# Three complement masks of a head made by adding transfers, and a new order of source tiles on the matmul engine

## The reference, cut to what matters

```python
seq = (x @ W_seq).reshape(N, H, DH)                    # N 2048, H 16, DH 32
scores = score1[:, :, None] + score2[:, None, :]
scores = leaky_relu(scores, negative_slope=0.2)
scores = scores + (1.0 - adj)[None, :, :] * MASK_VAL   # MASK_VAL -65500
attn = softmax(scores, axis=-1)
hidden = einsum('hij,jhd->ihd', attn, seq).reshape(N, D_IN)
```

## Time and profile before

| | |
|---|---|
| median of 3 runs | 1165.29 us (1164.87 to 1166.19) |
| the profiled execution | 1169.42 us, its span 1167.0 us |
| PE busy | 1080.7 us (93%) |
| DVE busy | 949.3 us (81%) |
| ACT busy | 809.0 us (69%) |
| POOL busy | 163.1 us (14%) |
| bytes moved | 77.69 MB, mean 67 GB/s |

### The profile page before, as it was taken

How to read it: one execution, slowest core, us unless ns; L and a number is a source line. 1 busy time by engine, 2 the same in 40 slices (tenths; PEclk the granted TensorE clock), 3 DMA queues, 4 the chain that set the end, 5 groups by cost and what they waited for, 6 DMA issues and landing times. The chain is left out here.

```text
span 1167.0 us, 24746 instructions
## 1 busy us (share of the span) xinstructions
PE 1080.7 (93%) x10565; PEld 738.8 (63%) x10565; DVE 949.3 (81%) x1323; ACT 809.0 (69%) x843; POOL 163.1 (14%) x174
## 2 busy tenths in 40 slices
PE   1999986999999999999996999999999999999997
PEld 1444432444444444444443999999999999999743
DVE  2355336899999999998834899999999999999565
ACT  1334326677777777775525999999999999999122
POOL 2788640000000000000000100100110000000011
PEclk9999996999999999999997899999999999999999
DMA  9630452322221121000433011110111111111311
GB/s 340 142 26 2 110 104 68 75 57 66 66 66 43 42 57 57 28 37 27 163 126 131 38 38 38 38 39 38 38 38 38 39 38 38 38 39 38 110 72 72
DMA packets 38269, 77.69 MB, mean 67 GB/s; under 512 B 5653, under 2 KB 15250, under 8 KB 36114
## 3 DMA queue, kind: packets, MB, share of 16 engines
q1 hardware_dynamic: 31954, 67.62, 16.1%
q0 software_dynamic: 6208, 8.50, 6.0%
HBM read 65.39 MB, written 23.21 MB: 76 GB/s over the span
## 5 line engine op out<-in xcount | busy, mean ns | idle before, releaser
L1443 ACT ACTIVATE area_h<-area_a,keep 128x2048 fp8e4<-128x2048 f32 x208 | 396.9, 1987 | 0.5 <-PEq L1577 0.5
L1595 PE MATMUL psum<-s_V,area_h 128*128 128x99 bf16 x2560 | 254.5, 210 | 21.1 <-issue 10.9
L1595 PEld LDWEIGHTS psum<-s_V,area_h 128*128 128x128 fp8e4 x2560 | 237.4, 98 | 25.2 <-issue 22.8
L1598 PE MATMUL psum<-s_V,area_h 128*128 128x198 bf16 x1536 | 218.7, 249 | 0.0
L1599 PE MATMUL psum<-s_V,late 128*128 128x99 bf16 x1536 | 212.8, 209 | 0.0
L1596 PE MATMUL psum<-s_V,area_b 128*128 128x99 bf16 x2048 | 205.5, 210 | 0.0
L1596 PEld LDWEIGHTS psum<-s_V,area_b 128*128 128x128 fp8e4 x2048 | 190.3, 98 | 0.0
L737 PE MATMUL psum<-area_h,f_region 128*128 128x512 f32 x384 | 184.9, 596 | 0.0
L1493 DVE TENSOR_TENSOR area_h<-area_h,area_a 128x512 uint32<-128x512 uint32 x256 | 173.5, 688 | 9.1 <-ACT area_h L1443 4.6
L1159 DVE SCALAR_TENSOR_TENSOR f_region<-area_b,s_r,f_region 128x1500 f32<-128x1500 f32 x96 | 170.8, 1780 | 2.2
L1170 DVE CUSTOM_DVE_ANT_0 area_b<-psum,late 128x1500 f32<-128x1500 f32 x96 | 161.1, 1715 | 10.8 <-PE psum L652 10.6
(11 more groups left out here) (175 smaller groups left out, 1343.5 us busy)
## 6 DMA issues: line engine op xcount, KB each, us to landing
area_a<-s_rows SPq DMA_DIRECT2D x16, 1024.0 KB, 4.6
rel_planes<-f_h SPq DMA_DIRECT2D x3, 2304.0 KB, 15.9
late<-rel_planes SPq DMA_DIRECT2D x36, 192.0 KB, 2.6
area_h<-in_x SPq DMA_DIRECT2D x4, 1024.0 KB, 12.9
keep<-in_adj POOLq DMA_DIRECT2D x16, 256.0 KB, 6.6
f_region<-in_x SPq DMA_DIRECT2D x16, 256.0 KB, 4.7
x<-f_region SPq DMA_DIRECT2D x16, 256.0 KB, 2.0
area_a<-adj_chunks SPq DMA_DIRECT2D x4, 1024.0 KB, 9.1
```

Of the source, the lines that this page charges most:

```text
L1443: act.activation(masks[:, j, :], s1b[:, b, :], ACT.Relu, bias=t["s2"][:, n, 0, j:j + 1], scale=BIG, saturate=False).then_inc(signs, 1)
L1595: pe.matmul(out[:, :, 0:DZ], masks[:, j, cols], V[:, b, j, :, 0:DZ], **first)
L1598: pe.matmul(out, masks[:, j, cols], V[:, b, j, :, :], **first)
```

## The change

Tiles 1, 6 and 10 get their complement from transfers. For each, and each head: SP copies the adjacency tile from a new DRAM tensor `far_rows` into the complement's buffer, once PE has used that buffer (`begin_far`); POOL, when DVE has masked the tile and that copy has landed, issues a transfer with addition that adds the mask onto it as 16-bit integers. In bytes 0x40 + 0x40 is 0x80, the fp8 value -0, and 0x40 + 0 stays 2.0, so what is left is the adjacency less the mask. For head 0 DVE makes the copies, and SP stores them from there into `far_rows`, ahead of stage 4.

FAR grows from 10 tiles to 12: 4 and 10 are new in it. DVE's complements are 0, 4, 7, 9, 11, 13, 14 (seven, before eight: 0, 1, 6, 7, 9, 11, 13, 14); POOL's stay 3 and 5. NEAR tiles are 2, 8, 12, 15 (before also 4 and 10), so `nadjT` has four tiles. PE takes the tiles in the order of `TURN`; ACT's and DVE's order stays 0 to 15, with waits for the place of a tile in `TURN`.

```diff
@@ stage 2, SP @@
+            for d, j in enumerate(DMA_FAR):
+                sp.wait_ge(t["apart"], d + 1)
+                sp.dma_start(t["far_rows"][d], t["fars"][FAR.index(j)]).then_inc(t["far_begun"][d], 16)
@@ stage 2, DVE, behind the loop of nadjT @@
+            for j in DMA_FAR:
+                dve.tensor_scalar(t["fars"][FAR.index(j)].bitcast(U32).rearrange("p (t i) -> p t i", t=NT),
+                                  t["adjT"][:, :, j, :].bitcast(U32), 0, None, ALU.bitwise_or).then_inc(t["apart"], 1)
@@ constants @@
-FAR = (0, 1, 3, 5, 6, 7, 9, 11, 13, 14)
+FAR = (0, 3, 4, 5, 7, 9, 11, 13, 14, 1, 6, 10)
 POOL_FAR = (3, 5)
-VECTOR_FAR = tuple(j for j in FAR if j not in POOL_FAR)
+DMA_FAR = (1, 6, 10)
+VECTOR_FAR = tuple(j for j in FAR if j not in POOL_FAR + DMA_FAR)
+TURN = (0, 2, 3, 4, 5, 7, 1, 8, 9, 11, 6, 12, 13, 14, 15, 10)
@@ stage 4, SP @@
-            for n in range(HB - 2):
-                sp.wait_ge(mask_ready, NT * (n + 1))
-                load(n + 2, n % 2)
+            def begin_far(n, d):
+                place = TURN.index(DMA_FAR[d])
+                if place < NT - 1:
+                    sp.wait_ge(mask_used, (NT - 1) * (n + 1) + place + 1)
+                else:
+                    sp.wait_ge(psum_done[1], n + 1)
+                sp.dma_start(fars[FAR.index(DMA_FAR[d])], t["far_rows"][d]).then_inc(far_begun[d], 16)
+            for n in range(HB - 1):
+                for d in range(len(DMA_FAR) - 1):
+                    begin_far(n, d)
+                if n < HB - 2:
+                    sp.wait_ge(mask_ready, NT * (n + 1))
+                    load(n + 2, n % 2)
+                begin_far(n, len(DMA_FAR) - 1)
@@ stage 4, POOL @@
-                for j in POOL_FAR:
+                for j in sorted(POOL_FAR + DMA_FAR):
                     pool.wait_ge(mask_ready, NT * n + j + 1)
-                    complement(pool, j, ALU.subtract).then_inc(pool_far, 1)
+                    if j in POOL_FAR:
+                        complement(pool, j, ALU.subtract).then_inc(pool_far, 1)
+                    else:
+                        d = DMA_FAR.index(j)
+                        pool.wait_ge(far_begun[d], 16 * (n + 1))
+                        pool.dma_start(fars[FAR.index(j)].bitcast(U16), masks[:, j, :].bitcast(U16), accum_op=ALU.add).then_inc(far_added[d], 16)
@@ stage 4, ACT (and the same in vector_sign on DVE) @@
-                        if j < NT - 1:
-                            act.wait_ge(mask_used, (NT - 1) * n + j + 1)
+                        if TURN.index(j) < NT - 1:
+                            act.wait_ge(mask_used, (NT - 1) * n + TURN.index(j) + 1)
@@ stage 4, PE @@
-            def step(n, b, half, j):
-                base = 4 * half
+            def step(n, b, half, place):
+                base, j = 4 * half, TURN[place]
                 if j in POOL_FAR:
                     pe.wait_ge(pool_far, len(POOL_FAR) * n + POOL_FAR.index(j) + 1)
+                elif j in DMA_FAR:
+                    pe.wait_ge(far_added[DMA_FAR.index(j)], 16 * (n + 1))
```

More of the change, by code:

```diff
@@ L21 @@
 U8 = mybir.dt.uint8
+U16 = mybir.dt.uint16
 F8 = mybir.dt.float8e4
@@ L1389, in stage4 @@
     pool_far = sem("pool_far")
+    far_begun = t["far_begun"]
+    far_added = [sem(f"far_added{d}") for d in range(len(DMA_FAR))]
     summed, scaled, joined, inverse = sem("summed"), sem("scaled"), sem("joined"), sem("inverse")
@@ L1481, in vector_sign @@
             def vector_sign(n, b, j):
-                dve.wait_ge(mask_used, (NT - 1) * n + j + 1)
+                dve.wait_ge(mask_used, (NT - 1) * n + TURN.index(j) + 1)
                 dve.wait_ge(s1_in[b], 8 * (n - b) + 16)
@@ L1577, in _ @@
             pe.sem_inc(mask_used, NT - 1)
-            def step(n, b, half, j):
-                base = 4 * half
-                if j == 0:
+            def step(n, b, half, place):
+                base, j = 4 * half, TURN[place]
+                if place == 0:
                     pe.wait_ge(bank_free[half], n + 1)
@@ L1591, in step @@
                     out = ps[:, base + i // 2, 256 * (i % 2):256 * (i % 2) + 3 * CZ].rearrange("p (s c) -> p s c", s=3)
-                    first = dict(start=(j == 0 and i % 2 == 0), stop=False, skip_group_check=True)
-                    then = dict(start=False, stop=(j == NT - 1), skip_group_check=True)
+                    first = dict(start=(place == 0 and i % 2 == 0), stop=False, skip_group_check=True)
+                    then = dict(start=False, stop=(place == NT - 1), skip_group_check=True)
                     if j in FAR:
@@ L1599, in step @@
                         last = pe.matmul(out[:, :, DZ:CZ], nadjT[:, NEAR_TILES.index(j), cols], V[:, b, j, :, DZ:CZ], **then)
-                if j == NT - 1:
+                if place == NT - 1:
                     last.then_inc(psum_done[half], 1)
-                if half and j < NT - 1:
+                if half and place < NT - 1:
                     last.then_inc(mask_used, 1)
@@ L1735, in build @@
         "s1_rows": dram("s1_rows", [HB, N]), "seq_rows": dram("seq_rows", [N, D]),
-        "adj_chunks": dram("adj_chunks", [NT, P, N], F8),
+        "adj_chunks": dram("adj_chunks", [NT, P, N], F8), "far_rows": dram("far_rows", [len(DMA_FAR), P, N], F8),
     }
@@ L1746, in build @@
         t["adjT_in"], t["seq_in"] = (c.enter_context(nc.semaphore(n)) for n in ("adjT_in", "seq_in"))
+        t["apart"] = c.enter_context(nc.semaphore("apart"))
+        t["far_begun"] = [c.enter_context(nc.semaphore(f"far_begun{d}")) for d in range(len(DMA_FAR))]
         t["rstd"] = c.enter_context(nc.sbuf_tensor("rstd", [P, 2, NT], F32))
```

## The result

Twenty executions each: median 1170.88 us after (1165.02 to 1173.84) against 1166.12 before (1160.47 to 1171.62); the medians differ by 4.8 us. The ratio, which is that of the means, is 1.0031 with a 95% interval of 1.0016 to 1.0047, so 3.6 us slower (1.9 to 5.5). Forecast were 1.1 us faster. The profiled executions are 1170.67 us after (span 1168.9) and 1169.42 before (1167.0).

A forecast was written before the change was run, and what follows sets the result against it. DVE bound the kernel at 28.20 us a head; afterwards a ring of DVE and PE would, at 27.97. Gains of 2.1 less 0.4 and 0.6 make 1.1 us faster, 1164.2 us; range 1157 to 1171.

The forecast's parts named there:

- The projection behind the heads is untouched: Step for the stretch after the last head: the change alters nothing there, so no time was added or taken.
- 2.4 around: Time of an execution outside its span: 2.4 us, added to the span of 1167.0 to give 1169.42.
- 1157 to 1171: Outer range in us for the whole kernel, taking in the DVE and POOL rivals, leaving out most late accumulates.
- the forecast's own range, 1161 to 1166.5: Range in us for the whole kernel if the forecast case holds, 0.2 us a head either way; chance 0.45.
- Head 0, "0.4 lost": First head, held by ACT's complement 11: its closing sum comes at 676.27 against 675.89, 0.4 us lost.
- The ring, 27.97: Steady heads: second sum, complement 11, PE from place 9, next second sum; 12.11 + 0.83 + 14.81 + 0.22 = 27.97 us period.
- The last head, 27.33 and 0.6 lost: Last head: PE hangs on complement 7, ending 27.33 us after head 14's sum against 26.69, 0.6 lost.
- Accumulates at cost 0: POOL's adding transfers: issue plus landing about 5 us, with 11.8 us allowed for tile 6, so no cost.
- DVE alone: Rival for the steady heads: DVE alone sets a period of 27.60 us, 6.6 us faster, 1158.7; chance 0.18.
- POOL against DVE: Rival at mask 6's end: POOL's descriptor writing holds up DVE's vector_sign, 0.5 us a head, 1171 us; chance 0.14.
- ACT waited: ACT writing tile 1: waits for place 6, 3 us at first, settling at most 1.2 us a head, cost 0.
- Complement 5 on POOL: Steady heads: it now meets DVE's complement 4; half a microsecond is covered, as PE wants tile 5 some 2 us later.

The follow-up runs named there:

- e2: The kernel before, with POOL issuing 48 more transfers in the heads that nothing uses, 45 of them adding; ratio 1.0045.
- e5: The kernel after with only tiles 6 and 11 exchanged in PE's order (11 at place 10); 1165.58 us in a single execution.
- e6: The kernel after with only tiles 1 and 7 exchanged in PE's order (7 at place 6); 1168.43 us in a single execution.
- e7: The kernel before, with POOL running 48 one-column memsets in the heads, with the same waits as e2's unused transfers; 1163.63 us in a single execution.
- e1: The kernel after with two exchanges in PE's order, tiles 1 and 7 and tiles 6 and 11; 1160.81 us, ratio 0.9952 to the kernel before.

## Why the prediction was wrong, step by step

- **The step that failed: "The projection behind the heads is untouched", which took everything from the last head to the end of the span at no change.** The projection is untouched (66.42 and 66.43 us), but the end behind it is not: 3.95 us, in no term and no rival. The transfers stood in the sum with POOL's time and their landing alone; e2 shows that issuing 48 of them lengthens the end by 3.9 us with nothing else changed. This one term turns 0.1 us faster into 3.8 slower. The "2.4 around" the span was taken as unchanged too, and came out at 1.8.
- **The outer range held by luck.** 1170.88 us lies inside "1157 to 1171" only because that range made room for POOL holding up DVE, which did not happen; the forecast's own range, 1161 to 1166.5, missed.
- **Head 0, "0.4 lost": 1.92 lost.** Place 9 came where the step had it, to 0.01 us; the 14.81 us behind it were taken at the full clock, and 1.53 more came from its fall. Steps were priced by a head at clock 1.00, though PE stalls twice in head 0.
- **The ring, 27.97: 27.93.** Its terms stand in the trace: complement 11 at s + 12.11 (12.11), handover 0.84 (0.83), the waits 1.13 and 0.48 (1.2 and 0.6), the sum's wait 0.23. The 14 periods gained 2.66 (2.1). The period of before is 28.21 by its rows, where the step has 28.20. e5 and e6 show that it is this ring and no other.
- **The last head, 27.33 and 0.6 lost:** 27.29 and 0.60; e6 shows that tile 7 is its cause.
- **Accumulates at cost 0:** issue of 0.86 to 1.02 us, landing after 3.4, against the 5 taken for both together and the 11.8 allowed. PE never waited for one. By the Trainium skill (Collectives: The Full Stack, The bandwidth ceiling, with the fit of DMA: Bandwidth & Descriptors, Anatomy of one DMA) it was an estimated 3.2, and the trace's 3.4 is near it.
- **Rivals.** DVE alone did not set the period in this kernel, but one exchange of two tiles makes it (e5). POOL against DVE: they do meet at tile 6, and DVE loses nothing, as vector_sign takes 1.28 us there as before. POOL is the one held: its issue of 790.55 starts 0.39 us behind vector_sign (the prediction had 0.1) and ends 0.13 behind its end, in 1.02 us instead of 0.86. e7 shows the hold bare, with memsets of 0.10 us; the one beside vector_sign takes 1.18 us and ends with it (rows below). ACT waited 1.25 us a head for place 6 (forecast 1.2) and held nobody.
- Complement 5 on POOL took 1.65 us instead of 1.28 where it met DVE's, and that was covered, as forecast.

Vector_sign and the memset beside it in e7, then the next memset of that head:

```profile
785.78 1.28 DVE L1492 TENSOR_SCALAR area_h<-area_a,keep 128x2048 fp8e4<-128x2048 f32 x1
785.92 1.18 POOL L1430 MEMSET s_dump<- 128x1 f32 x1 [1.27 <-DVE area_h L1501]
...
791.90 0.10 POOL L1430 MEMSET s_dump<- 128x1 f32 x1 [4.80 <-DVE area_h L1501]
```

By the rule of the Trainium skill (SBUF — State Buffer, Who interferes with whom) that the prediction cites, the later of the two is blocked for the whole of the other's instruction; these rows agree, POOL being let go 0.04 us behind vector_sign's end.

## What to carry to other kernels

When two engines take the same tiles in different orders, write down for every tile the time it is made and the time it is wanted, and close the ring: one tile one place too early cost this kernel 0.33 us a head. Look behind the last instruction as well: the stretch to the end of the span grew with each transfer that POOL was given here, and with the output stores on SP's queue it was short again. A stall in a first, unsettled iteration can cost more than its length, by the clock behind it.

## What the runs showed of the hardware that was not expected

- Each transfer added to POOL, whatever its size (1 or 256 KB) and kind, lengthened the end by 0.082 us while POOL issued the last stores; 48 memsets did not.
- PE's clock fell behind a wait of 2.06 us in head 0, with one of 1.93 us ahead of it, and in e6 behind one of 3.22 us. It did not fall behind one of 1.74 us in e1, nor with the waits of 1.13 and 0.48 us in each later head.
- An adding transfer holds POOL longer than a plain one: 0.86 us against 0.54 for 256 KB, and 0.76 for 1 KB. Beside vector_sign, which holds POOL until it ends, all of them take about 1.0. The plain ones landed after 2.7 us, the adding ones into DRAM after 4.1, those into on-chip memory after 3.4.
